# A graph network layer: running sums of edge features on 64 or on 128 lanes

## The reference

```python
edge_index = jnp.stack([src, dst])
# layer 0
aggregated = jax.ops.segment_sum(edge_attr, col, num_segments=x.shape[0])    # col = dst
inputs = jnp.concatenate([x, aggregated, u[batch]], axis=1)
h = swish(inputs @ W1 + b1)
x = layernorm(x + swish(h @ W2 + b2))
# layer 1: keys and values of each edge from x[src], edge_attr and 9 harmonics,
# softmax over each node's edges, weighted sum, projection, batch norm, layer norm
```

## Time and profile before

| | us |
|---|---|
| median of three runs | 2944.01 |
| lowest and highest | 2944.01, 2948.17 |
| profiled execution | 2940.88 |
| its span | 2938.7 |
| busy: DVE | 2590.5 (88%) |
| busy: PE | 2457.7 (84%) |
| busy: POOL | 1911.2 (65%) |
| busy: ACT | 1518.8 (52%) |

### The profile page before, as it was taken

How to read it: one execution, slowest core, us unless ns; L and a number is a source line. 1 busy time by engine, 2 the same in 40 slices (tenths; PEclk the granted TensorE clock), 3 DMA queues, 4 the chain that set the end, 5 groups by cost and what they waited for, 6 DMA issues and landing times. The chain is left out here.

```text
span 2938.7 us, 48472 instructions
## 1 busy us (share of the span) xinstructions
PE 2457.7 (84%) x12897; PEld 1776.8 (60%) x12897; DVE 2590.5 (88%) x3389; ACT 1518.8 (52%) x2914; POOL 1911.2 (65%) x1719
## 2 busy tenths in 40 slices
PE   2233358999999999999999999999999999999714
PEld 1232325667766666777677776777777777777511
DVE  6688735899999999999899999999999999999737
ACT  1321224565656655666565665666666666666410
POOL 2700037777777777777777777777777777777130
PEclk8555558999999999999999999999999999999855
DMA  6787713244444445444444444544444544544440
GB/s 187 211 221 189 208 27 103 75 128 145 145 143 143 140 140 149 145 142 146 141 142 145 143 145 140 148 144 146 145 147 142 147 144 145 145 146 141 120 139 11
DMA packets 229767, 415.36 MB, mean 141 GB/s; under 512 B 61999, under 2 KB 89059, under 8 KB 225830
## 3 DMA queue, kind: packets, MB, share of 16 engines
q1 hardware_dynamic: 169638, 296.66, 32.6%
q0 software_dynamic: 52704, 107.19, 14.9%
q10 hardware_dynamic: 7128, 8.13, 0.8%
HBM read 309.59 MB, written 102.20 MB: 140 GB/s over the span
## 5 line engine op out<-in xcount | busy, mean ns | idle before, releaser
L749 POOL DMA_INDIRECT gathered<-xtab_d,src_g x784 | 886.9, 1131 | 297.6 <-issue 216.6
L749 POOL DMA_INDIRECT gathered<-qtab_d,dst_g x784 | 877.6, 1119 | 254.5 <-issue 245.2
L1127 PE MATMUL bank<-z_h,wt_h 128*128 128x512 f32 x1568 | 729.1, 465 | 38.0 <-DVE val L1586 34.3
L879 ACT ACTIVATE z_h<-xa_t 128x512 fp32r<-128x512 f32 x980 | 616.7, 633 | 104.5 <-DVE xa_t L1553 77.1
L1553 DVE TENSOR_TENSOR xa_t<-bank,r_r 128x512 f32<-128x512 f32 x980 | 667.2, 682 | 1.7 <-PE bank L1155 1.7
L1129 PE MATMUL bank<-z_h,wt_l 128*128 128x512 f32 x1568 | 619.7, 395 | 0.0
L1128 PE MATMUL bank<-z_l,wt_h 128*128 128x512 f32 x1568 | 618.9, 395 | 0.0
L1561 DVE TENSOR_TENSOR z_l<-xa_t,z_h 128x1024 fp32r<-128x1024 f32 x392 | 476.6, 1216 | 43.9 <-ACT z_h L879 43.8
L1127 PEld LDWEIGHTS bank<-z_h,wt_h 128*128 128x128 f32 x1568 | 300.1, 191 | 145.6 <-issue 109.9
L1155 PE MATMUL bank<-s,sel 128*128 128x512 bf16 x980 | 349.2, 389 | 8.8 <-issue 4.3
L873 ACT ACTIVATE hid<-bank,b1kv 128x512 f32<-128x512 f32 x196 | 135.1, 689 | 407.2 <-PE bank L1111 407.2
(11 more groups left out here) (222 smaller groups left out, 4210.9 us busy)
## 6 DMA issues: line engine op xcount, KB each, us to landing
nrow_d<-x_r SPq DMA_DIRECT2D x196, 288.0 KB
ea<-in_ea_t SPq DMA_DIRECT2D x392, 128.0 KB
exb<-exd_d SPq DMA_DIRECT2D x196, 256.0 KB
dmb<-exd_d SPq DMA_DIRECT2D x196, 256.0 KB
ea_c<-in_ea_t SPq DMA_DIRECT2D x49, 512.0 KB, 5.0
aggrow_d<-xa_t SPq DMA_DIRECT2D x49, 512.0 KB, 3.9
gathered<-xtab_d,src_g POOLq DMA_INDIRECT x784
gathered<-qtab_d,dst_g POOLq DMA_INDIRECT x784
```

The costliest lines, as they stand in the source:

```text
L749: rows_in = pool.indirect_dma_start(rows[:, c % 4, k, :], None, table, bass.IndirectOffsetOnAxis(ap=picked[:, s, at:at + 1], axis=0))
L879: act.activation(z_h[:, c % 2, i, :], z[:, i, :], ACT.Copy).then_inc(zh_ok, 1)
L1127: pe.matmul(ps[:, :], wt_h[rows, w, :], high, start=start, stop=False)
```

## The change

The edge list is cut into two halves of EH = 50,176 edges. The features of the first half lie on lanes 0 to 63 and those of the second on lanes 64 to 127, and one scan runs along both; there are 28 chunks of W = 1792 columns. Each chunk needs two loads of features and two of flags. The scan is now (feature + state) x keep, with `keep` shifted by one edge, so that the state behind an edge is zero if the next edge has another node. PE turns every fourth column only (4 transposes of 112 columns per chunk), ACT copies one bank, and SP stores 448 rows of two sums to `sums_d`.

A node's sum is put together from three things: the stored sum in front of the quad of edges in which its last edge lies (gathered as before, but by `lead_i`, and masked by `led`); its own edges of that quad, which 25 new gathers on GpSimd fetch from the row-wise edge table (`quads`, 128 rows of 1 KB each) and DVE masks (`mine`) and adds; and, for the one node whose edges cross the middle of the list, the last sum of the first half (`mid_b`). `quads` shares its memory with `shf`, so these gathers wait for the third conversion. GpSimd's gathers move into both branches of its test for an unsorted list.

The order changes too. SP loads the first features before the flags are out, stores `keep` before it loads the harmonics and `x`, and no longer fetches `piece_last` and `line_i`; ACT does. The first two scans stand between the seven comparisons, `row_i` comes ahead of the cuts, and ACT's copies stand between its conversions. PE and ACT get a wait for the cuts before the node stage. Some semaphores are merged, mostly in the branch for unsorted lists, which doesn't run here. The sizes and the main parts of the diff:

```diff
-W = 2048
-NC = EP // W
+EH = EP // 2
+W = 1792
+NC = EH // W
 CR = 2
 CL = (NC - 2) // CR
-WJ = W // P
+CQ = 4
+WJ = 4
+WP = W // (CQ * WJ)
+KEEP_AT = 63
...
+            def load_edges(c, b):
+                lo = c * W
+                for half in range(2):
+                    sp.dma_start(ea_c[half * D:(half + 1) * D, b, :], edges_t[:, bass.ds(lo + half * EH, W)]
+                                 ).then_inc(chunk_in[b], 16)
+
+            def load_keeps(c, b):
+                lo = c * W
+                for half in range(2):
+                    sp.dma_start(keep_c[half * D:(half + 1) * D, b, :],
+                                 keep_d[bass.ds(lo + half * EH + KEEP_AT + 1, W)].rearrange("(o w) -> o w", o=1)
+                                 .to_broadcast([D, W])).then_inc(chunk_in[b], 16)
+
+            def load_chunk(c, b):
+                sp.wait_ge(chunk_run, c - (CR - 1))
+                load_edges(c, b)
+                load_keeps(c, b)
+
+            def store_chunk(c, b):
+                sp.wait_ge(chunk_row, c + 1)
+                sp.dma_start(sums_d.rearrange("(r h) d -> r (h d)", h=2)[bass.ds(c * (W // CQ), W // CQ), :]
+                             .rearrange("(p j) d -> p (j d)", p=WP), row_c[:, b, :]).then_inc(chunk_out[b], 16)
+
+            load_edges(0, 0)
+            sp.wait_ge(flags_done, 1)
...
+            sp.wait_ge(flags_out, 32)
+            load_keeps(0, 0)
+            load_edges(1, 1)
+            load_keeps(1, 1)
...
+            sp.wait_ge(chunk_out[0], 16 * ((NC + 1) // 2))
+            sp.wait_ge(chunk_out[1], 16 * (NC // 2))
+            sp.dma_start(mid_b[:, :], sums_d[EH // 2 - 2:EH // 2 - 1, :].to_broadcast([P, D])).then_inc(mid_in, 16)
...
+                pool.wait_ge(quad_ok, 2)
+                pool.wait_ge(split_done, 3)
+                for t in range(NT):
+                    pool.indirect_dma_start(quad_rows[:, t, :, :].rearrange("p i w -> p (i w)"), None,
+                                            edge_rows.rearrange("(r i) w -> r (i w)", i=CQ),
+                                            bass.IndirectOffsetOnAxis(ap=quad_i[:, t:t + 1], axis=0)
+                                            ).then_inc(quads_in, 16)
+                pool.wait_ge(chunk_out[0], 16 * ((NC + 1) // 2))
+                pool.wait_ge(chunk_out[1], 16 * (NC // 2))
+                for t in range(NT):
+                    pool.indirect_dma_start(x_r[:, t, D:2 * D], None, sums_d[:, :],
+                                            bass.IndirectOffsetOnAxis(ap=lead_i[:, t:t + 1], axis=0)
+                                            ).then_inc(ends_in[t * P // G], 16)
...
+            split(0)
             rows_out(0, 0)
             rows_out(1, 1)
-            with act.Fori(0, (NC - 3) // 2) as i:
+            split(1)
+            rows_out(2, 0)
+            rows_out(3, 1)
+            split(2)
+            with act.Fori(1, NC // 2 - 1) as i:
...
+                for j in range(WJ):
+                    tr = pe.transpose(bank[b][0:WP, j * P:(j + 1) * P],
+                                      run_c[:, b, bass.ds(CQ * j + CQ - 1, WP, CQ * WJ)], ident[:, :])
...
+                dve.tensor_tensor_scan(run_c[:, b, :], ea_c[:, b, :], keep_c[:, b, :], run_c[:, 1 - b, W - 1:W],
+                                       ALU.add, ALU.mult).then_inc(chunk_run, 1)
+
+            dve.wait_ge(zeroed, 5)
             for k in range(RP):
+                if k == 3:
+                    run(0)
+                if k == 5:
+                    run(1)
...
+            run(NC - 6)
+            run(NC - 5)
+            dve.wait_ge(quads_in, 16 * NT)
+            run(NC - 4)
+            dve.tensor_tensor(flat, flat, across(mine[:, :, :].rearrange("p t i -> p (t i)"), D, 1), ALU.mult
+                              ).then_inc(quad_step, 1)
+            dve.tensor_tensor(led[:, :], mine[:, :, 0], quad_f[:, :], ALU.mult).then_inc(led_ok, 1)
+            run(NC - 3)
+            dve.wait_ge(quad_step, 10)
+            for i in range(2):
+                dve.tensor_tensor(edges_of[:, :, i, :], edges_of[:, :, i, :], edges_of[:, :, 2 + i, :], ALU.add
+                                  ).then_inc(quad_step, 1)
+            run(NC - 2)
+            dve.wait_ge(quad_step, 12)
+            dve.tensor_tensor(edges_of[:, :, 0, :], edges_of[:, :, 0, :], edges_of[:, :, 1, :], ALU.add
+                              ).then_inc(quad_step, 1)
+            run(NC - 1)
+            dve.wait_ge(mid_in, 32)
+            dve.wait_ge(quad_step, 9)
+            dve.tensor_tensor(edges_of[:, :, 1, :], mid_b[:, :].rearrange("p (o d) -> p o d", o=1)
+                              .to_broadcast([P, NT, D]), across(mid_m[:, :], D, 1), ALU.mult).then_inc(quad_step, 1)
+            dve.wait_ge(quad_step, 14)
+            dve.tensor_tensor(edges_of[:, :, 0, :], edges_of[:, :, 0, :], edges_of[:, :, 1, :], ALU.add
+                              ).then_inc(quad_step, 1)
...
+                dve.tensor_tensor(x_r[:, tiles, D:2 * D], x_r[:, tiles, D:2 * D], across(led[:, tiles], D, 1), ALU.mult
+                                  ).then_inc(led_ok, 1)
+                dve.wait_ge(led_ok, n + 2)
+                dve.tensor_tensor(x_r[:, tiles, D:2 * D], x_r[:, tiles, D:2 * D], edges_of[:, tiles, 0, :], ALU.add
                                   ).then_inc(masked, 1)
```

More of the change, by code:

```diff
@@ L801, in _, with split @@
             act.activation(head_sel[:, BP - H:BP], headones[:, bass.ds(0, H, DH)], ACT.Copy).then_inc(head_ok, 1)
-            act.wait_ge(sh_in, 16)
-            for part in range(3):
+            def split(part):
                 if part > 0:
@@ L1033, in _ @@
             pe.matmul(bank[5][0:D, 448:449], w1u[:, :], u0[:, :], start=True, stop=True).then_inc(b1e_ps, 1)
-            pe.wait_ge(cuts, 1)
-            pe.matmul(bank[6][:, 0:PIECES], ones[0:1, :], l_line, start=True, stop=True).then_inc(cuts_ps, 1)
             pe.wait_ge(find_step, 4)
@@ L1040, in chunk_rows @@
                 pe.wait_ge(chunk_run, c + 1)
-                for h in range(2):
-                    if not isinstance(c, int) or c >= 2:
-                        pe.wait_ge(chunk_row, (c - 1) * 2)
-                    for j in range(8):
-                        tr = pe.transpose(bank[2 * b + h][:, j * D:(j + 1) * D],
-                                          run_c[:, b, bass.ds(8 * h + j, P, WJ)], ident[0:D, 0:D])
-                        if j == 0:
-                            carry(tr, consts_in, ALL_CONSTS)
-                    tr.then_inc(chunk_ps, 1)
+                if not isinstance(c, int) or c >= 2:
+                    pe.wait_ge(chunk_row, c - 1)
+                for j in range(WJ):
+                    tr = pe.transpose(bank[b][0:WP, j * P:(j + 1) * P],
+                                      run_c[:, b, bass.ds(CQ * j + CQ - 1, WP, CQ * WJ)], ident[:, :])
+                    if j == 0:
+                        carry(tr, consts_in, ALL_CONSTS)
+                tr.then_inc(chunk_ps, 1)
             chunk_rows(0, 0)
             chunk_rows(1, 1)
-            with pe.Fori(0, (NC - 3) // 2) as i:
+            pe.wait_ge(cuts, 1)
+            pe.matmul(bank[6][:, 0:PIECES], ones[0:1, :], l_line, start=True, stop=True).then_inc(cuts_ps, 1)
+            with pe.Fori(0, (NC - 2) // 2) as i:
                 for r in range(2):
                     chunk_rows(i * 2 + (2 + r), r)
-            chunk_rows(NC - 1, 0)
-            pe.wait_ge(chunk_row, 2 * NC)
+            pe.wait_ge(chunk_row, NC)
+            pe.wait_ge(cuts, 6)
             def turn_inputs(n, lo, w):
@@ L1463, in _ @@
             dve.tensor_reduce(within[:, :], rows[0], AX_X, ALU.add).then_inc(find_step, 1)
-            dve.tensor_reduce(has[:, :], rows[1], AX_X, ALU.max).then_inc(ends_ok, 1)
+            dve.tensor_reduce(own_f[:, :], rows[1], AX_X, ALU.add).then_inc(own_ok, 1)
+            dve.wait_ge(own_ok, 1)
+            dve.tensor_scalar(has[:, :], own_f[:, :], 1.0, None, ALU.min).then_inc(ends_ok, 1)
             dve.wait_ge(find_step, 9)
@@ L1488, in _ @@
+            dve.wait_ge(own_ok, 5)
+            dve.tensor_tensor(mine[:, :, :], across(iota_row[:, 0:CQ], NT, 2), across(own_f[:, :], CQ, 1), ALU.is_gt
+                              ).then_inc(own_ok, 1)
+            dve.wait_ge(own_ok, 6)
+            dve.tensor_tensor(mine[:, :, :], mine[:, :, :], not_past[:, :, :], ALU.mult).then_inc(own_ok, 1)
+            dve.wait_ge(own_ok, 7)
+            with dve.Fori(CL // 2, CL - 3) as i:
                 for r in range(CR):
                     run(2 + r, i)
-            for c in range(2 + CL * CR, NC):
-                run(c)
+            edges_of = quad_rows
```

266 lines of the change are left out of this document (147 added, 119 removed).

## The result

The changed kernel takes **2841.64 us** (median of three runs, 2840.13 to 2845.44) against 2944.01 before. The ratio is 0.965, with a 95% interval of 0.9628 to 0.9672. The forecast was 2838, with a range of 2806 to 2864. The profiled execution took 2840.13, its span 2838.3. Every ratio in this document is to the kernel before as timed beside the kernel in question, on the same chip.

What follows compares the result with a forecast made beforehand. The stage before the main loop was taken as bound by scans, the two-buffer load ring closely behind, turning transfer-bound. A gain of 111 us by the last scan, less 5 in the tail, took 2944 to 2838 us; range 2806 to 2864.

Steps and rivals of the forecast that it cites:

- Chunk 4: Way to the first chunks: with reordered scans and copies and 1 us for waits, chunk 4 starts at 78 instead of 112.
- Chunks 6 and 7: Early scan stage: the load of chunk 6 is issued at 82, lands 6 to 7 us later, so it starts at 89.
- 6.0 us a chunk: Loads in the scan stage: two DMAs of 64 lanes keep the 64-lane rate, so a chunk takes 6.0 us (4.6 to 6.6).
- rival (A): Scan stage: the two halves' loads overlap, the buffer ring is the bound, 4.7 us a chunk, 2819 us in all; chance 0.22.
- Quads' transfer: Late scan stage: gathering each node's last four edges moves 3.3 MB on the same DMA engines and adds 9 us.
- After chunk 24: End of the scan stage: four scans, a product and three sums take DVE 28.5 us; the last scan ends near 250.
- Tail: From last scan to main loop: middle node 2 to 3 us, sums behind masks 3, smaller store 1 less; 5 us lost.
- Gathers: GpSimd in the scan loop: gathers pass only in gaps between scans, two per chunk, just enough at both places DVE needs them.
- The sign at the loop's start: Main loop: its first multiply was to come at 348 us instead of 454, with the loop's length unchanged at 2286.
- (B): Scan stage: 6.0 to 6.5 us a chunk and both sets of gathers late, +10 and +12, so 2858 us; chance 0.22.
- (C): Main loop: PE left at a 1.2 GHz clock makes the kernel slower than before, up to 2988 us; chance 0.03.
- (D): Scan stage: loads of twice the lanes run slower than any seen, 8 us a chunk, 2882 us in all; chance 0.06.

## Why the prediction was right

The mechanism held, and so did the sum. That it hit the time within 4 us is in part luck: by chunk 16 the kernel was 10.5 us late, and the terms behind it gave more than half of that back.

- **Scans.** 3.92 us forecast, 3.95 measured.
- **Chunk 4**: 78 forecast, 81.1 measured (+3.1). SP held `reset_d`'s store for 19.4 us from 26.02 (the same store took 0.43 before; here the 4.4 MB loads of the harmonics and `x` were issued right ahead of it), so the load of chunk 2 was issued at 51.03; DVE waited 0.8 and 2.3 us for chunks 2 and 3. My 1 us for waits was too little. Chunk 0 was there in time.
- **Chunks 6 and 7.** The step "lands 6 to 7 us later, so it starts at 89" failed: its load was issued at 85.23 and used at 96.69, 11.5 later, and chunk 7 waited 3.6 more. Some 2 us of this are the ring's own, since a plain chunk takes 7.7 to 8.6 from issue to use. For the rest, the third part of the harmonics, 1.8 MB, was sent off at 87.43 into the middle of it; at the 355 GB/s of that stretch it takes 5.1 us. I had placed the conversion on ACT but not its transfer. No run takes this store out, but the kernel with the copies last bears it out: there it is sent off at 80.29, before chunk 4's load, and chunks 6 and 7 wait 1.35 and 2.28 us instead of 7.11 and 3.59.
- **6.0 us a chunk**: 6.08. The rows of 64 lanes were the right price, and the lanes that a load reaches were the cause: interleaving them took the rate per unit of share from 235 to 322, though with two buffers the chunk only to 5.7. The term was read as transfer alone; the third buffer shows some 0.7 us of it to be the ring's. By the rule of the Trainium skill that stood against rival (A) ("SBUF — State Buffer", "Can I just issue two DMAs to hit both halves?": two such DMAs take turns), the changed kernel's trace agrees: 237 GB/s for both together, 236 for one. The runs set two bounds to it: two DMAs on interleaved lanes come near the rate of one on 128 (316 and 322), and halves with a third buffer rose to 268 GB/s per unit of share.
- **Finding the ends**: 18.2 forecast, 17.0 measured (144.46 to 161.49), and 0.4 of wait. By chunk 16 the kernel was 10.5 us late (174.49 for 164).
- **Quads' transfer**: 9 forecast on top of eight periods of 6.0, 57 in all; the eight measured periods are 52.9 (174.49 to 227.40). That gave 4 back. Against the same kernel without them it is about 7.
- **After chunk 24**: 28.5 forecast, 27.5 measured. Last scan's end: 250 forecast, 254.9 measured.
- **Tail**: 5 forecast, 4.9 measured. But the cost lies elsewhere in part: the middle node's 2 us are given back, and most of what stays lies between the masks, each now with a sum behind it: 7.25 us from one of the last five to the next instead of 6.8, 39.3 from first to last instead of 35.5.
- **Gathers.** The step "in the scan loop gathers pass in the gaps only ... two fit" undercounted. GpSimd's timeline in the changed kernel, for one chunk (scan from 110.21 to 114.16):

```profile
110.48 4.43 POOL L746 DMA_INDIRECT dst_rows<-dst_d,row_i  x1 [0.31 <-issue]
115.21 0.94 POOL L746 DMA_INDIRECT dst_rows<-dst_d,row_i  x1 [0.30 <-issue]
116.46 0.94 POOL L746 DMA_INDIRECT dst_rows<-dst_d,row_i  x1 [0.30 <-issue]
```

The gather that a scan holds ends too, and two pass in the gap: three a chunk. The last of the 25 for `dst_rows` was issued at 116.46, the last for the quads at 214.59, and DVE waited for neither.

**The sign at the loop's start.** "The loop's first multiply at 348 instead of 454" took the end of the stage for that multiply: the one of the earlier trace rows starts at 472.15, so 106 us less would be 366, and it was 371.35.

**Rivals.** (A) was wrong in its premise and in its price: adjacent halves do not reach 361 GB/s, and where the lanes interleave, the ring of two buffers takes 5.7 us a chunk, not 4.7. The time of (B) should have read 2860, by its own 10 and 12. (B) did not happen at 6.1 to 6.8 us a chunk, but is what every faster version ran into: 8.6 us with one DMA, 8.5 with even and odd lanes, 10.8 with a third buffer for halves, 8.6 and 19.2 with both. (C) did not happen: the loop took 2290.0 us at a granted clock of 0.99. (D) did not.

## What to carry to other kernels

When scans or products are spread over twice the lanes, put the parts on alternating lanes, so that each load reaches all of them, and then look at the ring. Here the lanes were worth 12 to 13 us; the third buffer let the scans run back to back, but paid little until DVE's wait for the gathers had scans in front of it. Before making a stage of two-input DVE instructions denser, count the gathers that GpSimd must get through beside it, one per instruction boundary and one more per 1.25 us of gap, and put work of DVE's own in front of the wait for them, so that what follows that wait is short. To rank versions, compare the start of the first instruction behind the changed stage, and learn its scatter from kernels that are the same up to there: here some 3 us, where the runs of one kernel scatter by 7. And follow the bulk transfers of the head as well as its instructions: in four traces the load that met a store of 1.8 MB was late.

## What the runs showed of the hardware beyond that

A fill by GpSimd of 128 x 6400 held a DVE instruction on 25 columns for 5.30 us instead of 0.17, while one with two inputs issued 0.1 us before it passed in 0.19. A DVE product over 6400 columns held one gather for 7.14 us. And a ring of loads has a price that no rate shows: with the engines at a share of 0.81, a 1.1 MB chunk still took 6.7 to 8.7 us from issue to use (four turns in the kernel with one DMA and two buffers), against 3.6 us at the 322 GB/s per unit of share.
